# Third attention: GpSimd sets the probabilities above the diagonal to zero for key chunks 1, 2 and 3; TensorE adds the mask for chunk 0 only

## The chip, the cores and the metric

The kernel runs on one core of one Trainium2 chip. The metric is the device time of one execution in microseconds; the time before is the median of three runs.

## The reference

A chain of layers over x (16 sequences of 512 tokens, 128 features): two kinds of attention, a recurrent layer, a Mamba layer, and two mixture-of-experts layers. The change concerns the last attention alone, which computes, for 16 heads of 8 features:

```python
Q, K, V = split_heads(x @ Wq), split_heads(x @ Wk), split_heads(x @ Wv)
Q, K = _rope(Q), _rope(K)
scores = jnp.einsum('bhqd,bhkd->bhqk', Q, K) / jnp.sqrt(jnp.float32(d_k))
causal = jnp.tril(jnp.ones((S, S), dtype=bool))
scores = jnp.where(causal[None, None], scores, -jnp.inf)
attn = jax.nn.softmax(scores, axis=-1)
out = jnp.einsum('bhqk,bhkd->bhqd', attn, V)
return out.transpose(0, 2, 1, 3).reshape(B, S, D) @ Wo
```

The layer behind it is a mixture of 8 experts with the two best chosen for each token. Finding the experts and sending the token rows to them (routing) is done while the attention runs.

## The kernel before

`attend` serves all three attentions. The first has a relative bias and a causal mask, the second is not causal, the third is causal without a bias (`causal and bias is None`); it runs from about 3520 us to 4150 us of the span. The second and third also carry the routing.

A block b is one sequence, a group n = 4b + g (g from 0 to 3) is four heads of it, as two pairs of two heads (r = 0, 1). There are 16 blocks and 64 groups. Scores are held with keys on the partitions and queries along the row. Keys come in four chunks of 128. Because of causality chunk c needs only queries from 128c on, so the causal tiles are: i = 0 chunk 0 (512 wide), i = 1 chunk 1 (384 wide), i = 2 chunk 2 (256) and chunk 3 (128) side by side. In each chunk the first 128 columns are the block on the diagonal, in which half of the entries has to be masked.

A step of TensorE (`step`) does one group. It has six places, at = 3 x pair + i. At each it issues the transposed scores of group n (`scores_t`, L1409) with the mask behind them (L1427), then the plain scores of group n + 2 (`scores_s`, L1376), from which VectorE takes the row maxima (L1758), then one piece of the output of group n - 1 (`pv`, L1448): chunk 0 at the first two places, chunk 1 at the third and fourth, chunk 2 at the fifth, chunk 3 at the sixth. The mask is added by matmuls: identity times a matrix of -1e30 above the diagonal, in two halves of 64 rows, for the two heads side by side on halves of the array.

ScalarE takes the exponential of each tile from PSUM into `probs` (L1668), which is double buffered by group, and counts it in the semaphore `expd`. `pv` waits for the count of the last exponential of its chunk. The exponentials of group n wait for the output of group n - 2.

GpSimd's queue has, block by block: `values(b, g)`, a copy of V (L1303) for each group, and between them the routing of earlier blocks: `locate` (L572 to L582) and the first four scatters (`scatter`, L593, indirect DMAs) after the first `values`, four more scatters, `scale_logits` and `scale_rows` (L545 to L556) after the second, `choose` (L514 to L534) after the third, `stage_x` (L1334) and `parts` (L563, L564) after the fourth. `locate` and `scatter` of b - 3 begin with b = 3, scaling, `choose` and `parts` of b - 2 with b = 2, `stage_x` with b = 1. `parts` waits for ScalarE's logarithm `norm_log`, which is queued in the last step of a block behind its fifth place. SP's queue loads the operands of each group and waits, before it overwrites `v_raw`, for the `values` copy of two groups before.

Of the kernel before, what the change touches and what calls it, by code (L numbers as in the profile page):

```python
# [24 lines left out]
P = 128  # L25
# [1059 lines left out]
def attend(core, x, stacks, v_dram, shift_dram, w, scale, causal, bias=None, routed=None):  # L1085
# [41 lines left out]
    def exp_no(group, pair, i, r):  # L1127
        later = 1 if (pair, i) == LATE else 0
        return USES_OF_GROUP * (group + later) + 2 * EXP_ORDER.index((pair, i)) + r + 1
# [5 lines left out]
        return 2 * len(BY_POOL) * group + 2 * sorted(BY_POOL).index((pair, i)) + r + 1  # L1135

    TURNS = [(0, 1)] if causal else [(0,), (1,)]

    def bank(v, g, pair, i, r):
        return (USES_OF_GROUP * (4 * v + g) + 2 * NTILE * pair + 2 * i + r) % RING  # L1140

    with core.phase() as ph:
# [28 lines left out]
        misc_mm = ph.sem("misc_mm")  # L1171
        misc_read = ph.sem("misc_read")
        rt = Routing(ph, x, *routed) if routed else None
        late_mm = ph.sem("late_mm")
        shift_ready = ph.sem("shift_ready")
        inverted = ph.sem("inverted")
        block = ph.block()
# [108 lines left out]
        @block.gpsimd  # L1286
        def _(pool):

            pool.memset(t_k[:, :, :, :], 1.0).then_inc(zeroed, 1)
            pool.memset(v_st[:, :, :, :, :], 0.0).then_inc(zeroed, 1)  # L1290
            pool.wait_ge(zeroed, 2)
            for two in range(2):
                at = 2 * DK * two + DK
                pool.memset(v_st[:, two, :, :, at:at + 1], 1.0).then_inc(zeroed, 1)
            pool.wait_ge(zeroed, 4)
            pool.sem_inc(v_ready, 2)

            def values(b, g):
                n = 4 * b + g
                pool.wait_ge(v_loaded[g % 2], 16 * (2 * b + g // 2) + 16)  # L1300
                pool.wait_ge(pv_mm, n + 1)
                at = 2 * DK * (g % 2)
                pool.tensor_copy(v_st[:, g % 2, :, :, at:at + DK], v_raw[:, g % 2]).then_inc(v_ready, 1)  # L1303

            def add_bias(b, g, pair, i):

                (_, width, c, first), = tiles[i]
                for r in range(2):
                    j = 2 * pair + r
                    pool.wait_ge(t_copied, pool_no(4 * b + g, pair, i, r))  # L1310
                    tile = probs[:, g % 2, j, tile_at[i]:tile_at[i] + width]
                    pool.tensor_tensor(tile, tile, bias["t_whole"][:, 4 * g + j, first - c * P:first - c * P + width],  # L1312
                                       ALU.add).then_inc(t_biased, 1)

            if not rt:
                for b in range(NB):
                    for g in range(4):
                        values(b, g)
                        for pair, i in sorted(BY_POOL):
                            add_bias(b, g, pair, i)  # L1320
                return
            no = [0]

            def then(ins):
                no[0] += 1
                ins.then_inc(rt.pool_step, 1)
                pool.wait_ge(rt.pool_step, no[0])

            def stage_x(m, added, read):

                pool.wait_ge(misc_read, added + 1)
                if read is not None:
                    pool.wait_ge(misc_mm, read + 1)
                pool.tensor_copy(rt.staged_x[:, :], x[:, T * m:T * m + T]).then_inc(rt.x_staged, 1)  # L1334

            rt.empty_rows(pool)
            for b in range(NB):
                values(b, 0)
                if b >= 3:
                    rt.locate(pool, then, b - 3)  # L1340
                    rt.scatter(pool, b - 3, 0, 4)
                values(b, 1)
                if b >= 3:
                    rt.scatter(pool, b - 3, 4, 8)
                if b >= 2:
                    rt.scale_logits(pool, b - 2)
                    rt.scale_rows(pool, b - 2)
                values(b, 2)
                if b >= 2:
                    rt.choose(pool, then, b - 2)  # L1350
                values(b, 3)
                if b >= 1:
                    stage_x(b - 1, use_no(b, 2, "WO"), use_no(b, 0, "RB") if b >= 2 else None)
                if b >= 2:
                    rt.parts(pool, b - 2)
            rt.locate(pool, then, NB - 3)
            rt.scatter(pool, NB - 3, 0, 8)
            rt.scatter(pool, NB - 2, 0, 8)
            rt.scatter(pool, NB - 1, 0, 8)
            for u in range(RING_ROWS):  # L1360
                pool.wait_ge(rt.sent[u], 16 * TOPK * QT * (NB // RING_ROWS))

        @block.tensor
        def _(pe):
# [31 lines left out]
            def scores_t(b, v, g, pair, i, heads):  # L1396
                if pair == 0 and i == 0 and 0 in heads:
                    pe.wait_ge(t_loaded[g % 2], 96 * (2 * b + g // 2) + 96)
                banks = [bank(v, g, pair, i, r) for r in range(2)]
                for r in heads:  # L1400
                    t_bank_free(b, g, pair, i, r)
                for piece, (at, width, c, first) in enumerate(tiles[i]):
                    last = piece == len(tiles[i]) - 1
                    masked = causal and bias is None and first == c * P
                    parts = 3 if bias is not None and (pair, i) not in BY_DVE | BY_POOL else 0
                    out = [t_ps[:, banks[r], at:at + width] for r in range(2)]
                    for r in heads:
                        rows = slice(HALF * r, HALF * r + ROWS + SHIFT_ROWS)
                        mm = pe.matmul(out[r], t_k[rows, g % 2, pair, c * P:(c + 1) * P],  # L1409
                                       t_q[rows, g % 2, pair, first:first + width],  # L1410
                                       start=True, stop=not masked and not parts)
                        if last and not masked and not parts:
                            mm.then_inc(t_mm, 1)
                    for q in range(parts):
                        for k in range(2):
                            for r in heads:
                                rows = slice(HALF * r, HALF * r + HALF)
                                done = q == 2 and k == 1
                                mm = pe.matmul(out[r], bias["flip"][rows, k],
                                               bias["t"][q][rows, k, 2 * g + pair, first - c * P:first - c * P + width],  # L1420
                                               start=False, stop=done)
                                if last and done:
                                    mm.then_inc(t_mm, 1)
                    for k in range(2 if masked else 0):
                        for r in heads:
                            rows = slice(HALF * r, HALF * r + HALF)
                            mm = pe.matmul(out[r][:, 0:P], w["ident16"][rows, k], w["mask_t"][rows, k],  # L1427
                                           start=False, stop=(k == 1))
                            if last and k == 1:
                                mm.then_inc(t_mm, 1)  # L1430

            def pv(b, k, c, at, to):
                n, g = 4 * b + k, k % 4
                if bias is None and causal and c < 3:
                    pe.wait_ge(expd, exp_no(n, 1, c, 1))
                if not causal and c == 0:
                    pe.wait_ge(expd, USES_OF_GROUP * (n + 1))
                if bias is not None and c < 2:
                    pe.wait_ge(expd, min(max(exp_no(n, pair, c, 1) for pair in range(2)), USES_OF_GROUP * GROUPS + 2))
                if bias is not None and c == 2:  # L1440
                    pe.wait_ge(expd, max(exp_no(n, pair, 2, 1) for pair in range(2)))
                if c == 0:
                    pe.wait_ge(v_ready, 2 + n + 1)
                    if g % 2 == 0:
                        pe.wait_ge(evacuated, 2 * b + g // 2 + 1)
                first = c * P if causal else 0
                for j in range(4):
                    mm = pe.matmul(o_ps[32 * j:32 * j + 32, at:to], v_st[:, g % 2, c, j, :],  # L1448
                                   probs[:, g % 2, j, place[c] + at - first:place[c] + to - first],
                                   start=(g % 2 == 0 and c == 0 and at == 0),  # L1450
                                   stop=(g % 2 == 1 and c == 3 and to == T))
                if c == 3 and to == T:
                    mm.then_inc(pv_mm, 1)
# [1372 lines left out]
```

## Time and profile before

| | us |
|---|---|
| median of three runs | 4495.58 (4492.27 to 4496.21) |
| the profiled execution | 4488.49 |
| its span | 4486.7 |
| busy in the span: TensorE, VectorE, ScalarE, GpSimd | 3969.0, 3190.9, 2844.3, 2366.9 |
| third attention, steady part (3700 to 4050): TensorE, VectorE, ScalarE, GpSimd | 331.6, 307.2, 254.7, 210.0 of 350 |

Busy time of TensorE overlaps with that of its weight loads. Spans of instructions on one engine can overlap their neighbours slightly, so costs in a row are best read from start to start.

### The profile page before, as it was taken

The numbers are of one execution on the slowest core, as the hardware profiler recorded it, in microseconds if no ns is written. First come the engines' busy times: TensorE is split into PE (matmuls) and PEld (weight loads), VectorE is DVE, ScalarE is ACT, GpSimd is POOL, SyncE is SP. The second block draws the span as 40 slices with busy tenths as digits, with TensorE's granted clock in tenths as the row PEclk, the third lists the DMA queues.
The fourth block names the chain that finished last, engine by engine and source line by source line (L and its number), as shares of the span: only waits on it lengthen the run. The fifth ranks groups of instructions, "written<-read, shape, count | busy, mean of one in ns | idle before, by whom it ended". The sixth has DMA issues, their size and how long they took to land. (4 is left out here: it accounts for less than half of the span.)

```text
span 4486.7 us, 91792 instructions
## 1 busy us (share of the span) xinstructions
PE 3969.0 (88%) x30019; PEld 2002.6 (45%) x30020; DVE 3190.9 (71%) x7556; ACT 2844.3 (63%) x5771; POOL 2366.9 (53%) x2903
## 2 busy tenths in 40 slices
PE   7699999899688989889889999997988699996997
PEld 4244444463233333337323333336974244443896
DVE  3588888547899999984479999972126788886013
ACT  7488888767565555547758888873324477775332
POOL 3366666311599999970413444544545246556452
PEclk8799999999899999999979999998989799998997
DMA  9533333104533333310543333325665544442665
GB/s 276 176 90 87 87 88 87 28 0 160 187 131 133 119 126 134 132 64 0 183 148 90 88 89 90 92 68 168 213 207 180 165 112 110 117 113 79 205 213 197
DMA packets 515891, 564.61 MB, mean 126 GB/s; under 512 B 162498, under 2 KB 435523, under 8 KB 507280
## 3 DMA queue, kind: packets, MB, share of 16 engines
q1 hardware_dynamic: 497312, 521.88, 37.9%
q0 software_dynamic: 18160, 37.42, 2.3%
q8 instruction: 229, 3.75, 0.4%
q14 instruction: 190, 1.56, 0.1%
HBM read 399.39 MB, written 159.68 MB: 125 GB/s over the span
## 5 line engine op out<-in xcount | busy, mean ns | idle before, releaser
L1668 ACT ACTIVATE p_probs<-p_t_ps 128x512 f32<-128x512 f32 (+1 forms) x2048 | 1029.4, 557 | 336.2 <-PE p_t_ps L1427 144.9
L1448 PE MATMUL p_o_ps<-p_probs,p_v_st 128*32 128x256 f32 (+3 forms) x9728 | 748.9, 381 | 10.0 <-ACT p_o_sb L1630 9.4
L1761 DVE TENSOR_REDUCE p_row_max<-p_s_ps 128x1 f32<-128x512 f32 x1024 | 632.4, 677 | 51.1 <-PE p_s_ps L1376 51.0
L1376 PE MATMUL p_s_ps<-p_s_k,p_s_q 48*128 48x512 bf16 (+3 forms) x3072 | 607.9, 334 | 52.3 <-DVE p_row_max L1758 36.9
L2492 POOL TENSOR_TENSOR xn<-p_dtx,p_b_sb 128x512 f32<-128x512 f32 x512 | 633.5, 1271 | 34.4 <-DMA p_b_sb<-mamba_rows 17.4
L2564 DVE TENSOR_TENSOR_SCAN p_state<-p_da,xn 128x1024 f32<-128x1024 f32 x256 | 578.8, 2276 | 9.7 <-ACT p_da L2430 7.8
L1409 PE MATMUL p_t_ps<-p_t_q,p_t_k 50*128 50x512 bf16 (+3 forms) x3072 | 546.4, 333 | 36.3 <-ACT p_probs L1668 10.5
L2430 ACT ACTIVATE p_da<-p_dt,p_rate 128x512 f32<-128x512 f32 (+1 forms) x512 | 331.9, 679 | 279.5 <-DVE p_state L2564 277.8
L1758 DVE CUSTOM_DVE_ANT_0 p_tried<-p_s_ps,c_mask_row 128x512 bf16<-128x512 f32 (+3 forms) x1024 | 441.0, 485 | 79.6 <-PE p_s_ps L1376 72.7
L1758 DVE CUSTOM_DVE_ANT_0 p_tried<-p_s_ps,p_s_bias 128x512 bf16<-128x512 f32 (+3 forms) x1024 | 441.4, 481 | 76.0 <-PE p_s_ps L1376 74.4
L1312 POOL TENSOR_TENSOR p_probs<-p_probs,xn 128x384 f32<-128x384 f32 (+1 forms) x384 | 409.1, 1096 | 148.7 <-ACT p_probs L1666 148.3
L802 POOL DMA_INDIRECT weighed_rows<-p_y,p_raw x284 | 272.5, 959 | 290.7 <-DVE p_y L790 246.3
L2340 PE MATMUL p_y_ps<-p_prod,c_ident 128*128 128x512 f32 x832 | 419.5, 627 | 3.8 <-DVE xn L2580 3.7
L790 DVE TENSOR_TENSOR p_y<-p_out_ps,p_raw 128x256 f32<-128x256 f32 x142 | 60.3, 425 | 503.5 <-PE p_out_ps L741 503.5
L772 ACT ACTIVATE p_hidden<-p_hid_ps 128x512 f32<-128x512 f32 x284 | 169.6, 597 | 316.7 <-PE p_hid_ps L730 316.6
L1409 PEld LDWEIGHTS p_t_ps<-p_t_q,p_t_k 50*128 50x128 bf16 x3072 | 166.6, 93 | 445.7 <-ACT p_probs L1668 229.3
L1448 PEld LDWEIGHTS p_o_ps<-p_probs,p_v_st 128*32 128x32 f32 x9728 | 193.9, 108 | 308.4 <-issue 256.1
L1376 PEld LDWEIGHTS p_s_ps<-p_s_k,p_s_q 48*128 48x128 bf16 x3072 | 213.7, 94 | 227.3 <-DVE p_row_max L1761 126.4
L593 POOL DMA_INDIRECT routed_rows<-p_rows,p_index x256 | 252.3, 986 | 99.8 <-issue 72.3
L1303 POOL COPY p_v_st<-p_v_raw 128x128 f32<-128x128 f32 x192 | 56.1, 292 | 439.4 <-PE p_o_ps L1448 251.4
L741 PE MATMUL p_out_ps<-p_wb,p_hidden 128*128 128x128 f32 x2272 | 276.6, 275 | 0.0
L730 PE MATMUL p_hid_ps<-p_xt,p_wb 128*128 128x256 f32 x1136 | 272.6, 384 | 0.0
(318 smaller groups left out, 7018.9 us busy)
## 6 DMA issues: line engine op xcount, KB each, us to landing
p_wb<-in_w SPq DMA_DIRECT2D x142, 512.0 KB, 3.5
p_b_sb<-mamba_rows SPq DMA_DIRECT2D x64, 1024.0 KB
p_s_q<-stack_q SPq DMA_DIRECT2D x384, 96.0 KB, 2.3
p_s_k<-stack_k SPq DMA_DIRECT2D x384, 96.0 KB, 2.4
p_t_q<-stack_q SPq DMA_DIRECT2D x384, 96.0 KB
p_t_k<-stack_k SPq DMA_DIRECT2D x384, 96.0 KB
p_raw<-routed_rows SPq DMA_DIRECT2D x142, 130.0 KB, 3.2
stack_q<-p_parts SPq DMA_DIRECT2D x48, 384.0 KB, 2.6
```

The source lines that it names most:

```text
L741: mm = pe.matmul(out_ps[:, j % 2, c * P:(c + 1) * P], hidden[:, j % 2, f, c * P:(c + 1) * P], wb[:, j % WB, FFN + f * P:FFN + (f + 1) * P] ...
L1312: pool.tensor_tensor(tile, tile, bias["t_whole"][:, 4 * g + j, first - c * P:first - c * P + width], ALU.add).then_inc(t_biased, 1)
L1376: mm = pe.matmul(s_ps[:, slot, at:at + width], s_q[rows, g % 2, pair, c * P:(c + 1) * P], s_k[rows, g % 2, pair, 0:width], start=True, sto ...
L1409: mm = pe.matmul(out[r], t_k[rows, g % 2, pair, c * P:(c + 1) * P], t_q[rows, g % 2, pair, first:first + width], start=True, stop=not mask ...
L1448: mm = pe.matmul(o_ps[32 * j:32 * j + 32, at:to], v_st[:, g % 2, c, j, :], probs[:, g % 2, j, place[c] + at - first:place[c] + to - first] ...
L1668: act.activation(exps, tile, ACT.Exp, scale=scale).then_inc(expd, 1)
L1758: read = dve.tensor_tensor_reduce(tried[:, slot, at:at + width], scores, over, 1.0, LOWEST, ALU.add, ALU.max, found)
L1761: read = dve.tensor_reduce(found, scores, X, ALU.max)
L2340: pe.matmul(y_ps[:, h], w["ident"], prod[:, prod_slot(u, n), half(h)], start=(n == 0), stop=(n == STATE - 1)).then_inc(acc_mm, 1)
L2430: act.activation(da[:, n % RA, h * T + h:h * T + T], dt[:, u, h, h:T], ACT.Exp, scale=rate[:, h, n:n + 1]).then_inc(da_ready, 1)
L2492: pool.tensor_tensor(dbx[:, n % R, half(h)], dtx[:, u, h], b_sb[:, n % RB], ALU.mult).then_inc(dbx_ready, 1)
L2564: dve.tensor_tensor_scan(out=state[:, n % RS], data0=da[:, n % RA], data1=dbx[:, n % R], initial=0.0, op0=ALU.mult, op1=ALU.add).then_inc( ...
```

## The change

For the third attention the diagonal blocks of chunks 1, 2 and 3 (tiles i = 1 and 2, `CLEARED`) are no longer masked before the exponential. GpSimd sets the entries above the diagonal of the finished exponentials to zero with `affine_select`, in place in `probs`, eight instructions for each group: one for each tile i = 1 (128 columns) and one for each tile i = 2 (the two diagonal blocks, 2 x 128 columns), for two pairs and two heads. Each waits for its tile's count in `expd` and counts itself in `cleared`. `clear(n)` stands in GpSimd's queue before the first `values` of the next block (groups 4b - 1) and before the second, third and fourth `values` (groups 4b, 4b + 1, 4b + 2). `pv` of chunk 1 waits for six of the eight, that of chunk 2 for all eight; chunk 3 follows chunk 2. Chunk 0 keeps its mask matmuls.

```diff
+    CLEARED = (1, 2) if causal and bias is None else ()
...
+            def clear(n):
+                if not CLEARED or n < 0:
+                    return
+                for pair, i, r in itertools.product(range(2), CLEARED, range(2)):
+                    pool.wait_ge(expd, exp_no(n, pair, i, r))
+                    last = 2 * (len(tiles[i]) - 1)
+                    blocks = probs[:, n % 2, 2 * pair + r, tile_at[i]:tile_at[i] + (last + 1) * P]
+                    blocks = blocks.rearrange("p (k q) -> p k q", q=P)[:, 0:last + 1:2]
+                    pool.affine_select(blocks, blocks, [[0, len(tiles[i])], [1, P]], ALU.is_ge, 0.0, base=0,
+                                       channel_multiplier=-1).then_inc(cleared, 1)
...
             for b in range(NB):
+                clear(4 * b - 1)
                 values(b, 0)
                 if b >= 3:
                     rt.locate(pool, then, b - 3)
                     rt.scatter(pool, b - 3, 0, 4)
+                clear(4 * b + 0)
                 values(b, 1)
...
+                clear(4 * b + 1)
                 values(b, 2)
                 if b >= 2:
                     rt.choose(pool, then, b - 2)
+                clear(4 * b + 2)
                 values(b, 3)
...
+            clear(GROUPS - 1)
...
-                    masked = causal and bias is None and first == c * P
+                    masked = causal and bias is None and first == c * P and i not in CLEARED
...
-                if bias is None and causal and c < 3:
+                if bias is None and causal and c < 1:
                     pe.wait_ge(expd, exp_no(n, 1, c, 1))
+                if CLEARED and c in CLEARED:
+                    pe.wait_ge(cleared, 8 * n + 4 + 2 * c)
```

GpSimd's order in the third attention, in a late block, from the last instruction of `locate` to the end of the scaling. Before:

```order
L582 COPY p24_rows<-p24_part 128x8
L593 DMA routed_rows<-p24_rows,p24_index 69376x130 x4
L1303 COPY p24_v_st<-p24_v_raw 128x16x8
L593 DMA routed_rows<-p24_rows,p24_index 69376x130 x4
L545 TENSOR_TENSOR p24_logits<-p24_raw,p24_rstd 128x32
L555 TENSOR_TENSOR p24_rows<-p24_raw,p24_rstd 128x4x128 x2
L556 COPY p24_rows<-p24_table_home 128x8
```

After (the `values` copy is now L1304, the select L1338):

```order
L582 COPY p24_rows<-p24_part 128x8
L593 DMA routed_rows<-p24_rows,p24_index 69376x130 x4
L1338 AFFINE_SELECT p24_probs<-p24_probs 128x128 x2
L1338 AFFINE_SELECT p24_probs<-p24_probs 128x2x128 x2
L1338 AFFINE_SELECT p24_probs<-p24_probs 128x128 x2
L1338 AFFINE_SELECT p24_probs<-p24_probs 128x2x128 x2
L1304 COPY p24_v_st<-p24_v_raw 128x16x8
L593 DMA routed_rows<-p24_rows,p24_index 69376x130 x4
L545 TENSOR_TENSOR p24_logits<-p24_raw,p24_rstd 128x32
L555 TENSOR_TENSOR p24_rows<-p24_raw,p24_rstd 128x4x128 x2
L556 COPY p24_rows<-p24_table_home 128x8
```

The eight selects of a group stand between the first four scatters and the `values` copy, behind which come the other four scatters and the scaling. The selects of the next group follow the scaling.

TensorE's order around the third place of a step of the third attention (scores of tile 2, then the first output piece of chunk 1). Before:

```order
L1448 MATMUL p24_o_ps<-p24_probs,p24_v_st 32x256 x4
L1463 MATMUL p24_misc<-c_ident,p24_row_max 16x128
L1409 MATMUL p24_t_ps<-p24_t_q,p24_t_k 128x256 x2
L1427 MATMUL p24_t_ps<-c_mask_t,c_ident16 128x128 x4
L1409 MATMUL p24_t_ps<-p24_t_q,p24_t_k 128x128 x2
L1427 MATMUL p24_t_ps<-c_mask_t,c_ident16 128x128 x4
L1376 MATMUL p24_s_ps<-p24_s_k,p24_s_q 128x256 x2
L1448 MATMUL p24_o_ps<-p24_probs,p24_v_st 32x192 x4
```

After (the lines L1409, L1376, L1448 and L1463 are now L1426, L1393, L1467 and L1482):

```order
L1467 MATMUL p24_o_ps<-p24_probs,p24_v_st 32x256 x4
L1482 MATMUL p24_misc<-c_ident,p24_row_max 16x128
L1426 MATMUL p24_t_ps<-p24_t_q,p24_t_k 128x256 x2
L1426 MATMUL p24_t_ps<-p24_t_q,p24_t_k 128x128 x2
L1393 MATMUL p24_s_ps<-p24_s_k,p24_s_q 128x256 x2
L1467 MATMUL p24_o_ps<-p24_probs,p24_v_st 32x192 x4
```

Two sets of four mask matmuls are gone at this place, and the last row is the first that waits for the selects.

## Rows read from the trace of the kernel before

**Rows 1.** Windows of the third attention: us, busy of PE, PEld, DVE, ACT, POOL; PEclk; DMA

```profile
3700.00:4050.00 350.00, 331.63 (x4683) 163.14 (x4679) 307.17 (x1391) 254.70 (x649) 209.96 (x461) 1.00 0.42 115
...
3536.00:3575.00 39.00, 34.91 (x428) 15.97 (x429) 32.25 (x153) 24.22 (x51) 1.65 (x6) 0.79 0.43 112
...
4105.00:4170.00 65.00, 26.88 (x183) 19.88 (x180) 24.87 (x97) 15.87 (x51) 29.27 (x40) 0.63 0.30 96
```

**Rows 2.** Waits from 3536 to 4107 us: waiter, released by, us in total, times, longest

```profile
ACT p_probs L1668 <- PE p_t_ps L1427: 144.9, 251, 15.8
POOL p_v_st L1303 <- DMA p_v_raw<-values: 111.0, 46, 10.7
PEld p_t_ps L1409 <- ACT p_probs L1668: 104.5, 257, 0.9
POOL p_part_log L563 <- ACT p_norm_log L1611: 77.6, 14, 5.9
```

**Rows 3.** Timeline of TensorE, the last step of a block: start us, us, instruction

```profile
3813.93 0.39 PE L1409 MATMUL p_t_ps<-p_t_q,p_t_k 50*128 50x512 bf16 x2
...
3816.70 0.28 PE L1409 MATMUL p_t_ps<-p_t_q,p_t_k 50*128 50x256 bf16 x2
3816.82 0.28 PE L1427 MATMUL p_t_ps<-c_mask_t,c_ident 64*128 64x128 bf16 x4
3816.93 0.22 PE L1409 MATMUL p_t_ps<-p_t_q,p_t_k 50*128 50x128 bf16 x2
...
3817.31 0.53 PE L1448 MATMUL p_o_ps<-p_probs,p_v_st 128*32 128x192 f32 x8
...
3823.66 0.39 PE L1409 MATMUL p_t_ps<-p_t_q,p_t_k 50*128 50x512 bf16 x2
```

**Rows 4.** Timeline of GpSimd: one `locate` five blocks earlier, then one block

```profile
3644.11 1.05 POOL L572 TENSOR_TENSOR p_base<-p_base,p_counts 128x8 f32<-128x8 f32 x4 [0.53 <-ACT p_counts L1570]
...
3805.95 0.29 POOL L1303 COPY p_v_st<-p_v_raw 128x128 f32<-128x128 f32 x1 [0.17 <-DMA p_v_raw<-values]
...
3813.92 0.20 POOL L534 TENSOR_TENSOR p_behind<-p_best 128x4 f32<-128x4 f32 x1
...
3815.00 0.29 POOL L1303 COPY p_v_st<-p_v_raw 128x128 f32<-128x128 f32 x1 [0.87 <-DMA p_v_raw<-values]
3815.23 0.62 POOL L1334 COPY p_staged_x<-x 128x512 f32<-128x512 f32 x1
...
3821.26 0.20 POOL L563 TENSOR_TENSOR p_part_log<-p_behind,p_norm_log 128x4 f32<-128x4 f32 x1 [5.41 <-ACT p_norm_log L1611]
...
3824.50 1.05 POOL L572 TENSOR_TENSOR p_base<-p_base,p_counts 128x8 f32<-128x8 f32 x4
...
3828.05 0.20 POOL L582 COPY p_rows<-p_part 128x8 f32<-128x8 f32 x1 [0.47 <-ACT p_part L1618]
3829.07 1.06 POOL L593 DMA_INDIRECT routed_rows<-p_rows,p_index  x1 [0.82 <-POOL p_rows L582]
...
3833.92 0.31 POOL L1303 COPY p_v_st<-p_v_raw 128x128 f32<-128x128 f32 x1
...
3841.39 0.19 POOL L556 COPY p_rows<-p_table_home 128x8 int32<-128x8 int32 x1
```

**Rows 5.** GpSimd groups by shape, whole span: count, busy us, mean ns, idle before

```profile
L1303 POOL COPY p_v_st<-p_v_raw 128x128 f32<-128x128 f32 x192 | 56.1, 292 | 439.4 <-PE p_o_ps L1448 251.4 <-DMA p_v_raw<-values 187.8
...
L516 POOL TENSOR_SCALAR p_ahead<-p_differ 128x256 f32<-128x256 f32 x28 | 24.4, 870 | 2.5
...
L518 POOL TENSOR_TENSOR p_differ<-p_differ,p_table_earlier 128x256 f32<-128x256 f32 x28 | 20.4, 729 | 2.3
...
L1334 POOL COPY p_staged_x<-x 128x512 f32<-128x512 f32 x30 | 18.5, 617 | 0.8 <-DVE x L1814 0.6
...
L525 POOL TENSOR_SCALAR p_is_rank<-p_rank 128x32 f32<-128x32 f32 x56 | 16.1, 288 | 4.8
...
L521 POOL TENSOR_TENSOR p_half<-p_ahead 128x128 f32<-128x128 f32 x28 | 12.8, 457 | 2.2
```

More of the change, by code:

```diff
@@ L1173, in attend @@
         rt = Routing(ph, x, *routed) if routed else None
-        late_mm = ph.sem("late_mm")
+        late_mm, cleared = ph.sem("late_mm"), ph.sem("cleared")
         shift_ready = ph.sem("shift_ready")
```

## Prediction

> **What bounds the kernel now.** Only the third attention changes, so I read its stretch. Of the window table, the three rows in [rows 1] are the steady part, the start and the tail of this attention. In the steady part TensorE is busy 331.6 of 350 us (95%) at a granted clock of 1.00, VectorE 307.2, ScalarE 254.7 and GpSimd 210.0. The list of waits over the whole attention [rows 2] agrees: ScalarE waits 144.9 us for the mask matmuls of L1427, while weight loads of L1409 wait 104.5 us for exponentials, which is time that mostly lies beside running matmuls. TensorE sets the pace, with VectorE 8% behind it. GpSimd looks free: 40% idle. But its idle time is of one kind only, and that decides this case. Per block of four groups it is the wait for `norm_log` (77.6 us over 14 blocks), a wait for the `values` load, and gaps between its DMA issues, which are not free time.
>
> The pace: the first `base` addition of `locate` starts at 3644.11 and, five blocks later, at 3824.50 [rows 4]. That is 180.4 / 5 = 36.1 us for a block, 9.0 for a group.
>
> **What TensorE saves.** In the step at [rows 3] the two 256-wide score matmuls start at 3816.70, their masks at 3816.82, the next scores at 3816.93: four mask matmuls (two halves of the identity, two heads side by side) cost 0.11 us. A group has eight such sets, two for each key chunk; six go. That is 6 x 0.11 = 0.66 us of a group's 9.0, so a TensorE step of 8.4, and 64 x 0.66 = 42 us at the most, if nothing else becomes late. VectorE's 307.2 of 350 is 31.7 us of a 36.1 us block, still below 4 x 8.4 = 33.4, so it would not stop this gain.
>
> **What GpSimd gets.** Each group adds eight selects, four over 128x128 and four over 2x128 columns. No row shows such an instruction, so I bound the mean cost c of one (start to start) by what GpSimd does on float32 of these widths [rows 5]. From below: the copy, 0.292 us for 128 columns and 0.617 for 512, by interpolation 0.40 for 256, mean 0.35; back to back the next instruction starts some 0.05 before such a span ends (0.23 after the copy at 3815.00, [rows 4]), so c = 0.30. From above, within the rows: TENSOR_SCALAR with a comparison, 0.870 for 256 columns and 0.288 for 32, so 0.54 for 128, mean 0.70, c = 0.65. Between them TENSOR_TENSOR, 0.457 for 128 and 0.729 for 256, mean 0.59, c = 0.54. A select reads one operand, but makes a comparison value for each element and chooses by it, so I hold it nearer to the dearer rows and take c = 0.54. It could be dearer than all of them, since it also counts the positions; I keep 0.8 as the outer end.
>
> One sentence of the Trainium skill, "GPSIMD Engine Reference", section 4.1 (Engine selection), says that one-input elementwise work on GpSimd runs at roughly line rate; by that c would be the copy's 0.30 and the sum below about +22 us. The row speaks against its use here: the one-input comparison takes (0.870 - 0.288) / 224 = 2.6 ns for a column against the copy's (0.617 - 0.292) / 384 = 0.85.
>
> **Where the selects lie.** GpSimd runs its queue in order. The output matmuls of group n-1 for chunk 1 are issued at the third place of step n and now wait for the sixth select of group n-1, those for chunks 2 and 3 at the fifth place for the eighth. In the step of [rows 3] that third place is 3.4 us in (3813.93 to 3817.31). Selects of a group can't end before its exponentials, about when the next step begins, so GpSimd has only some 3 us in which it must be free, once in each step. Its old work is queued right in front of them: behind the change a block reads `values`, `locate`, four scatters, select group 4b; `values`, four scatters, scaling, select 4b+1; `values`, `choose`, select 4b+2; `values`, `stage_x`, `parts`, select 4b+3. Work that had 36 us to be done in is now waited for three times in a block.
>
> I follow one block around from S, the end of the sixth select of group 4b+2, at which TensorE goes on at the third place of the last step. Durations are from [rows 3, 4].
> - TensorE and ScalarE until `parts` can run: 3821.26 - 3817.31 = 3.95, less one mask set, 3.8; `parts` itself 0.4. The last two selects, `values` and `stage_x` hide in it (2 x 0.54 + 0.9 = 2.0). Together 4.2.
> - Eight selects of group 4b+3: 8c.
> - `values` 0.25, `locate` to its first scatter 3829.07 - 3824.50 = 4.57 less its 0.47 of waiting, 4.1; four scatters 3833.92 - 3829.07 = 4.85. Together 9.2.
> - Eight selects of group 4b: 8c. The sixth comes S + 4.2 + 9.2 + 14c = S + 21.0; TensorE without waiting would be there at S + 6.0 (3823.66 - 3817.31, less three mask sets) + 8.4 + 3.1 (the 3.4 to the third place, less three) = S + 17.5. It waits 3.5 us.
> - `values`, four scatters and scaling: 3841.58 - 3833.92 = 7.7. Then 8c. That leg is 12.0 where a TensorE step is 8.4: 3.6 us of waiting.
> - `values` and `choose`: 3814.12 - 3805.95 = 8.2 (the last row's start and its 0.20). Then 6c of group 4b+2, which is the next S. Again 12.5 against 8.4.
>
> The sum is 29.3 + 30c. With c = 0.54 a block takes 45.5 us instead of 36.1: +9.4. The chain is closed by GpSimd alone except for its first 3.8 us, so the 0.66 us of each TensorE step is lost in it, all but the one mask set counted. Scatters run from block 3 on: 13 blocks, 13 x 9.4 = +122 us. Of the eleven steps before the first S, TensorE saves 11 x 0.66 = 7 us, and block 2, which already has scaling and `choose`, gives back about 4 in its two waits: -3. The tail is as it was (24 scatters behind the last selects, [rows 1] third row, TensorE idle); I give it 0. ScalarE and VectorE are not charged. SP's queue waits for `values` before it reloads `v_raw`; each `values` now comes up to a step later, behind the selects of the group before, but still before the SP step that asks for it, so 0; were it late, the loads of t_q would be next and TensorE with them, which I leave to the upper end.
>
> Total: 122 - 3 = +119. The profiled execution took 4488.5 us (span 4486.7), which lies 7.1 below the median of the runs, 4495.6. So 4488.5 + 119 = 4607.5, and for the median 4615. At c = 0.30 a block is 38.3, +2.2, 13 x 2.2 = 29, with the full 7 saved ahead: +22, 4517. At c = 0.65: 48.8, 13 x 12.7 - 3 = +162, 4658. At c = 0.8: 13 x 17.2 - 3 = +221, 4717. No change of pace at 29.3 + 30c = 36.1, c = 0.23.
>
> **Rivals.**
> - Faster: the selects fit. It decides at c = 0.23, no more than the 128-column copy's own spacing of 0.23, and four of eight selects are twice as wide. For it speaks the 40% of idle GpSimd [rows 1]; against it that the chain above counts every gap and that a select can hardly beat a copy. If it all fitted: -42 us, 4453. Chance 0.07, and 0.04 for the narrow band around no change.
> - Cheap selects, at the copy's rate, c up to 0.42: TensorE loses what it saved and some; +22 to +72, about 4545. Chance 0.22.
> - My forecast, c from 0.42 to 0.68: +72 to +174. Chance 0.47.
> - Dear selects, or TensorE's clock. This stretch was granted 1.00, the 2.4 GHz level, throughout; at the start of this attention, where TensorE waits for loads and maxima, it is 0.79, and in the tail, where it mostly idles, 0.63 [rows 1]. Waits of 3 to 4 us three times a block may bring the 1.2 GHz level into the steady part. Most of that would be hidden by the waits themselves, but the 3.8 us leg in front of `parts` is on the chain and could double: 13 x 3.5 = +45, about 4660. With c near 0.8 the same. Chance 0.20.
> - That the masks don't go, or something else is added: the order of instructions shows 24 mask matmuls fewer in each step and eight selects more; no chance left for it.
>
> **How the numbers follow.** Likeliest 4615. The range leaves out about 0.1 on each side: below, the faster case and the cheapest selects, 4515; above, c over 0.79 or half clock on top of 0.65, 4710. About 0.2%, 9 us, is what a measurement here can tell from no change. Faster 0.07, same 0.04, slower 0.89.
>
> **What would show it.** In the new profile: mask matmuls at 512 instead of 2048; selects whose mean over the two widths is near 0.6 us; GpSimd busy over 85% of the steady stretch; blocks of about 45 us between first `base` additions; TensorE's output matmuls waiting for GpSimd's selects in three steps of four, not in the step after `parts`, and hardly at all in blocks 0 and 1, where steps should be 8.4 us. Wrong would be: selects under 0.25 us, waits in every step alike, or a block much longer than 29.3 + 30c, which would mean a link that I have left out (the clock, the reloading of `v_raw`, or GpSimd and VectorE slowing each other).

## The result, and the profile after

The change made the kernel slower: 4537.3 us median of four runs (4532.2 to 4541.9) against 4493.9, ratio 1.0096 with an interval of 1.0083 to 1.0109, or +43 us. A second measurement beside the later experiments gave 1.0103 (1.0088 to 1.0119). The direction and the mechanism were forecast, the size (+119) was not.

The profiled execution took 4541.9 us, span 4540.2, that is 53.5 more than the span before. Of these, 7.7 had come up before GpSimd's first routing instruction of this attention (3549.8 against 3542.1), in code that the change does not touch. I take them for scatter between executions: the first weighed-row scatter of the first expert layer (L802) starts at 3081.9 against 3076.2 here, and between 3076.2 and 3082.3 over the fourteen traces of this document. The line of busy times, and the window that answers to the first of [rows 1]:

```profile
PE 3987.0 (88%) x28483; PEld 1973.4 (43%) x28484; DVE 3189.1 (70%) x7556; ACT 2844.3 (63%) x5771; POOL 2518.5 (55%) x3415
```

```profile
3700.00:4050.00 350.00, 308.04 (x3397) 130.17 (x3395) 280.21 (x1265) 229.84 (x584) 275.80 (x702) 0.93 0.38 103
```

TensorE fell from 331.6 to 308.0 us busy of 350, GpSimd rose from 210.0 to 275.8, and the granted clock fell from 1.00 to 0.93. The selects, by shape in the same window, to be held against [rows 5]:

```profile
L1338 POOL TENSOR_SCALAR_AFFINE_SELECT p_probs<-p_probs 128x256 f32<-128x256 f32 x140 | 53.2, 401 | 0.0
L1338 POOL TENSOR_SCALAR_AFFINE_SELECT p_probs<-p_probs 128x128 f32<-128x128 f32 x140 | 37.6, 288 | 0.1
```

They take 0.29 and 0.40 us, the copy's own times (0.292, and 0.40 by interpolation). Eight in a row take 2.43 us from start to start, so c = 0.304. Waits from 3560 to 4150 us, as in [rows 2]:

```profile
ACT p_probs L1687 <- PE p_t_ps L1444: 100.5, 96, 3.1
...
PEld p_o_ps L1467 <- POOL p_probs L1338: 49.4, 44, 2.4
POOL p_part_log L563 <- ACT p_norm_log L1630: 41.8, 13, 4.0
PE p_o_ps L1467 <- POOL p_probs L1338: 40.6, 35, 2.2
POOL p_probs L1338 <- ACT p_probs L1687: 30.0, 31, 2.0
...
POOL p_v_st L1304 <- DMA p_v_raw<-values: 10.1, 9, 2.1
```

The output matmuls now wait for GpSimd. GpSimd's own waiting for the load of `values` has gone from 111.0 us in [rows 2] to 13.0 in the stretch that answers to it, 3544 to 4160; between 3700 and 4050 it has gone from 28.0 to nothing. The 30.0 us in which the selects wait for exponentials lie in the first three blocks; between 3700 and 4050 there are none. GpSimd's timeline over two blocks, which answers to [rows 4]:

```profile
3806.69 1.04 POOL L572 TENSOR_TENSOR p_base<-p_base,p_counts 128x8 f32<-128x8 f32 x4
...
3836.59 2.48 POOL L1338 TENSOR_SCALAR_AFFINE_SELECT p_probs<-p_probs 128x128 f32<-128x128 f32 x8
3839.02 0.29 POOL L1304 COPY p_v_st<-p_v_raw 128x128 f32<-128x128 f32 x1
3839.25 0.61 POOL L1346 COPY p_staged_x<-x 128x512 f32<-128x512 f32 x1
3842.08 0.20 POOL L563 TENSOR_TENSOR p_part_log<-p_behind,p_norm_log 128x4 f32<-128x4 f32 x1 [2.22 <-ACT p_norm_log L1630]
...
3845.11 1.04 POOL L572 TENSOR_TENSOR p_base<-p_base,p_counts 128x8 f32<-128x8 f32 x4
...
3877.49 0.29 POOL L1304 COPY p_v_st<-p_v_raw 128x128 f32<-128x128 f32 x1
...
3882.37 0.20 POOL L563 TENSOR_TENSOR p_part_log<-p_behind,p_norm_log 128x4 f32<-128x4 f32 x1 [4.04 <-ACT p_norm_log L1630]
...
3885.39 1.04 POOL L572 TENSOR_TENSOR p_base<-p_base,p_counts 128x8 f32<-128x8 f32 x4
```

One block is 38.42 us, the next 40.28, and so they alternate nearly throughout: the 13 intervals between the 14 first `base` additions have a mean of 39.30, where before it was 35.70. Of these 39.30, GpSimd is busy 32.96 and has 2.8 of gaps at its scatters; it waits 3.19 for `norm_log` and 0.32 for ScalarE's `part` in `locate`, and for nothing else. The wait for `norm_log` is 2.2 us in the shorter block, 4.0 in the longer. What differs is TensorE's clock in that leg. Its timeline, from the first output piece of chunk 1 in the last step of either block:

```profile
3838.40 0.53 PE L1467 MATMUL p_o_ps<-p_probs,p_v_st 128*32 128x192 f32 x8 [1.08 <-POOL p_probs L1338]
...
3841.06 0.64 PE L1467 MATMUL p_o_ps<-p_probs,p_v_st 128*32 128x256 f32 x8
...
3876.87 0.87 PE L1467 MATMUL p_o_ps<-p_probs,p_v_st 128*32 128x192 f32 x8 [2.23 <-POOL p_probs L1338]
...
3881.55 1.08 PE L1467 MATMUL p_o_ps<-p_probs,p_v_st 128*32 128x256 f32 x8
```

In the shorter block, after a wait of 1.08 us, the matmuls run at the 2.4 GHz level (0.53, 0.64); in the longer one, after a wait of 2.23 us, at 1.2 GHz (0.87, 1.08), until 3882.6. From that first piece to `parts` it is 3.68 us in the one and 5.50 in the other, which is the 1.8 us by which the blocks differ.

The shorter block has the half level too, but one step earlier, where TensorE waits for the next selects again. The same pieces of chunk 1 in the step before, first of the shorter block, then of the longer:

```profile
3827.88 0.72 PE L1467 MATMUL p_o_ps<-p_probs,p_v_st 128*32 128x192 f32 x8 [1.41 <-POOL p_probs L1338]
...
3829.71 0.87 PE L1467 MATMUL p_o_ps<-p_probs,p_v_st 128*32 128x192 f32 x8
...
3866.34 0.53 PE L1467 MATMUL p_o_ps<-p_probs,p_v_st 128*32 128x192 f32 x8 [1.42 <-POOL p_probs L1338]
```

Waits of 1.41 and 1.42 us stand in front, and only the first is followed by the half level. The alternation is not a fixed feature of the kernel: in a second profiled execution of the change the wait for `norm_log` also lies between 2.2 and 4.0 us, but mostly in between, and the mean block is 39.20.

### The profile page after: what moved, and what is told of

Its sections match the earlier page's. It is cut to its first block and busy times, and to the rows that moved or that the text cites. A ratio compares the mean times of both kernels' runs of the same rounds, so it can differ in the third digit from the quotient of the medians.

```text
span 4540.2 us, 89233 instructions
## 1 busy us (share of the span) xinstructions
PE 3987.0 (88%) x28483; PEld 1973.4 (43%) x28484; DVE 3189.1 (70%) x7556; ACT 2844.3 (63%) x5771; POOL 2518.5 (55%) x3415
## 5 line engine op out<-in xcount | busy, mean ns | idle before, releaser
L1467 PE MATMUL p_o_ps<-p_probs,p_v_st 128*32 128x256 f32 (+3 forms) x9728 | 763.4, 387 | 53.2 <-POOL p_probs L1338 42.9
L1393 PE MATMUL p_s_ps<-p_s_k,p_s_q 48*128 48x512 bf16 (+3 forms) x3072 | 637.9, 339 | 54.8 <-DVE p_row_max L1777 37.3
L2511 POOL TENSOR_TENSOR xn<-p_dtx,p_b_sb 128x512 f32<-128x512 f32 x512 | 633.0, 1271 | 34.8 <-DMA p_b_sb<-mamba_rows 17.9
L1426 PE MATMUL p_t_ps<-p_t_q,p_t_k 50*128 50x512 bf16 (+3 forms) x3072 | 537.5, 337 | 30.0 <-ACT p_probs L1687 8.9
L802 POOL DMA_INDIRECT weighed_rows<-p_y,p_raw x284 | 271.9, 957 | 291.9 <-DVE p_y L790 247.5
L1467 PEld LDWEIGHTS p_o_ps<-p_probs,p_v_st 128*32 128x32 f32 x9728 | 196.0, 109 | 359.7 <-issue 250.9
L1426 PEld LDWEIGHTS p_t_ps<-p_t_q,p_t_k 50*128 50x128 bf16 x3072 | 155.6, 93 | 447.4 <-ACT p_probs L1687 217.0
L1393 PEld LDWEIGHTS p_s_ps<-p_s_k,p_s_q 48*128 48x128 bf16 x3072 | 227.0, 96 | 260.9 <-DVE p_row_max L1780 126.4
L741 PEld LDWEIGHTS p_out_ps<-p_wb,p_hidden 128*128 128x128 f32 x2272 | 264.9, 192 | 0.1
```

The lines of the kernel that those rows point to most:

```text
L741: mm = pe.matmul(out_ps[:, j % 2, c * P:(c + 1) * P], hidden[:, j % 2, f, c * P:(c + 1) * P], wb[:, j % WB, FFN + f * P:FFN + (f + 1) * P] ...
L1393: mm = pe.matmul(s_ps[:, slot, at:at + width], s_q[rows, g % 2, pair, c * P:(c + 1) * P], s_k[rows, g % 2, pair, 0:width], start=True, sto ...
L2511: pool.tensor_tensor(dbx[:, n % R, half(h)], dtx[:, u, h], b_sb[:, n % RB], ALU.mult).then_inc(dbx_ready, 1)
```

## The experiments

Times are against the kernel before on the same chip. "Block" is the mean of the 13 intervals between first `base` additions in the profiled execution. "No masks, no selects" leaves out the masking of chunks 1 to 3 altogether.

| kernel | ratio (95% interval) | us | block |
|---|---|---|---|
| before | | | 35.70 |
| the change, again | 1.0103 (1.0088 to 1.0119) | +45 | 39.20 |
| masks kept as well | 1.0129 (1.0113 to 1.0144) | +56 | 39.75 |
| selects twice | 1.0384 (1.0368 to 1.0400) | +170 | 47.87 |
| two scatters moved | 1.0002 (0.9993 to 1.0011) | +1 | 35.88 |
| no masks, no selects | 0.9969 (0.9957 to 0.9982) | -14 | 34.99 |
| only tile 2 cleared | 0.9969 (0.9957 to 0.9981) | -14 | 34.82 |

**GpSimd's chain, stretched.** Each group's selects were done a second time:

```diff
-                for pair, i, r in itertools.product(range(2), CLEARED, range(2)):
+                for again in range(2):
+                    for no, (pair, i, r) in enumerate(itertools.product(range(2), CLEARED, range(2))):
...
-                    pe.wait_ge(cleared, 8 * n + 4 + 2 * c)
+                    pe.wait_ge(cleared, 16 * n + 12 + 2 * c)
```

> Each group's eight selects are done twice (the second pass changes nothing; TensorE waits for the second). Theory A: the block is 29.3 + 60 x 0.304 = 47.5 us, 9.1 more than the change, 13 x 9.1 = +118 and a few us in block 2: about +120 over the change, +165 over before; with the 1.2 GHz level after longer waits up to 45 us more. Rival B, that GpSimd has slack left and the change's loss comes from where TensorE has to wait rather than from how long GpSimd works: well under +80 over the change.

Measured +170, and the first `base` additions of one block and the next:

```profile
3801.15 1.06 POOL L572 TENSOR_TENSOR p_base<-p_base,p_counts 128x8 f32<-128x8 f32 x4
...
3848.93 1.05 POOL L572 TENSOR_TENSOR p_base<-p_base,p_counts 128x8 f32<-128x8 f32 x4
```

The blocks are 47.75 to 47.82 us, the last alone 48.94, against 47.5 from the formula. The selects are on the path one by one. The granted clock of the steady window was 0.87, and yet the block is no longer than the sum. TensorE's output pieces of chunk 1, and two of chunk 2 (256 wide), in three steps on end:

```profile
3814.33 0.87 PE L1470 MATMUL p_o_ps<-p_probs,p_v_st 128*32 128x192 f32 x8 [5.01 <-POOL p_probs L1341]
...
3826.80 0.53 PE L1470 MATMUL p_o_ps<-p_probs,p_v_st 128*32 128x192 f32 x8 [2.26 <-POOL p_probs L1341]
...
3829.46 1.08 PE L1470 MATMUL p_o_ps<-p_probs,p_v_st 128*32 128x256 f32 x8
...
3839.78 0.53 PE L1470 MATMUL p_o_ps<-p_probs,p_v_st 128*32 128x192 f32 x8 [2.30 <-POOL p_probs L1341]
...
3842.44 0.64 PE L1470 MATMUL p_o_ps<-p_probs,p_v_st 128*32 128x256 f32 x8
```

The half level (0.87, 1.08) falls into the first two legs, after which TensorE waits for the selects again anyway. The leg in front of `parts`, from 3839.78 on, runs at 2.4 GHz.

**GpSimd's chain, shortened where it was idle.**

```diff
-                    rt.scatter(pool, b - 3, 4, 8)
+                    rt.scatter(pool, b - 3, 4, 6)
...
                     stage_x(b - 1, use_no(b, 2, "WO"), use_no(b, 0, "RB") if b >= 2 else None)
+                if b >= 3:
+                    rt.scatter(pool, b - 3, 6, 8)
```

> The change with two of the second four scatters moved from in front of the selects of group 4b+1 to the last slot of the block, between stage_x and parts, where GpSimd waits 2.2 to 4.0 us for norm_log. Theory A, the chain of GpSimd: that slot grows to 0.6 + 0.9 + 0.2 + 2.5 + 0.4 = 4.6 us, the other shrinks by 2.5: 27.2 + 30 x 0.304 = 36.3 us a block, 2.1 less than 38.4; and the alternating 1.6 us, TensorE's half level in front of parts, is hidden behind the scatters. 13 x 0.6 - 2 = +6 us over before, some 37 us faster than the change. Rival, that only the sum of GpSimd's work counts or that waits at fixed places cost in themselves: as the change, +43.

Measured +1: 44 us came back by moving two scatters into the wait for `norm_log`, which fell from 3.2 us a block to 0.1. The clock of its steady window is 1.00 again. No select was saved and none got cheaper (0.288 and 0.400 us), so what the change lost could be had back by the order of GpSimd's queue alone. GpSimd now works almost without a break, busy 33.1 us and 2.7 of gaps at its scatters in a block of 35.9, and TensorE still waits for its selects 17 times between 3700 and 4050, 10.5 us in all. With the move the change is as fast as the kernel before, not faster.

**TensorE's part alone.** The masks of chunks 1 to 3 left out and no selects (`clear` returns at once, `pv` waits for `expd`).

> The masks of key chunks 1 to 3 left out and nothing in their place (leaves out the masking of these diagonal blocks; output not the reference's). It measures what TensorE's part is worth alone. Theory A: TensorE is the bound of the kernel before, six sets of 0.11 us in each of 64 steps: -42 us, block 35.7 - 2.6 = 33.1 us, granted clock still 1.00. Rival: VectorE (31.7 us of a block) with ScalarE's and the misc bank's waits is next at once: half of it, about -20 us.

Measured -14: the rival, and less than it said. So even free selects could not have brought 42 us. Its waits from 3700 to 4050 us:

```profile
PEld p_t_ps L1426 <- DMA p_t_q<-shifts: 15.0, 18, 1.9
PEld p_s_ps L1393 <- DVE p_row_max L1777: 11.4, 47, 0.6
```

Before the change these were 9.5 and 0.5 in the same window. The shifts are the row maxima with their sign turned, which go through a store and a load before they stand in `t_q` for the transposed scores. I took VectorE for the cause first.

**The change with its masks kept.** `masked = causal and bias is None and first == c * P`, selects as in the change.

> The change with all mask matmuls kept as well (the selects then clear entries that are zero already). Theory A, GpSimd's queue sets the block: at the measured 0.304 us a select a block is 29.3 + 30 x 0.304 = 38.4 us whatever TensorE does beside it, against 35.7 before, so +13 x 2.7 = +35 us over the kernel before; and since TensorE's gaps are filled with mask matmuls again, the drops of its granted clock (0.93 in the steady part of the change, every second block 40.2 us instead of 38.4) become fewer: +35 to +43, not slower than the change's +43. Rival B, TensorE's 0.66 us a group still counts in the change: this run is slower than the change by up to 42 us, +85 over before.

Measured +56, between both theories. Its blocks are 0.45 to 0.55 us longer than the change's, some 6 to 7 us in all; the rest of the 11 us is about as large as the uncertainty of two ratios from different chips. Theory B is out, theory A misses some 15 us: TensorE's work is not fully beside the chain. The traces tell what carries the 0.55 us a block over the second profile of the change: GpSimd waits 0.58 us a block for ScalarE's `part` in `locate` instead of 0.28, and 3.32 for `norm_log` instead of 3.16, and is busy 0.1 us longer. The granted clock was 0.96 in its steady window, higher than with the change (0.93 and 0.94), so more drops of the clock are not the reason.

**Half of the selects.** `CLEARED = (2,)`, with the counts of `cleared` to match.

> Only tile 2 (chunks 2 and 3) is cleared by GpSimd, four selects of 0.35 us start to start for each group; chunk 1 keeps its mask matmuls, so four of the six sets go. Theory A: GpSimd's chain is 29.3 + 15 x 0.35 = 34.6 us, below the 35.7 of before, TensorE's own block 35.7 - 1.8 = 33.9: block 34.6, 13 x -1.1 and three blocks of -1.8: -20 us against before, granted clock 1.00. Rival B, waits for GpSimd at fixed places cost whatever its load: slower than before.

Measured -14, block 34.8. From 3700 to 4050 us TensorE has no wait for GpSimd. But it is only what leaving out all masks brings, so something at 35.0 us a block was holding both.

**What holds 35.0 us.** VectorE's maxima were spread otherwise, on top of two kernels:

```diff
         s_tiles = [[(0, 512, 3)], [(0, 128, 0), (128, 384, 2)], [(0, 256, 1)]]
+        if bias is None:
+            s_tiles = [[(0, 512, 3)], [(0, 384, 2)], [(0, 256, 1), (256, 128, 0)]]
```

> As the kernel that clears only tile 2 (measured -14), with VectorE's maxima spread otherwise: query chunk 0 (128 keys) goes from the second and fifth place of the step to the third and sixth. Theory V, which explains why taking the masks away alone gave -14 and not -42: at the second and fifth place the four maxima of two heads take 2 x (0.21 + 0.48) = 1.38 us, as long as TensorE's place of 1.28 us, so time saved there is waited away for VectorE; moved, they take 0.96 there and 1.10 instead of 0.69 in the other. Then GpSimd's chain, 34.6 us, is next, against 35.0 now: about -20 over before. Rival, loads of shifted rows or ScalarE hold the block at 35.0: -14 again.

> Masks of chunks 1 to 3 and selects left out (output not the reference's), with the same new spread of VectorE's maxima. Theory V: TensorE's saving comes through, block near 33.5 us instead of 35.0, about -35 us over before (-14 without the new spread). Rival: -14 again.

Measured 0.9976 (0.9967 to 0.9985) and 0.9966 (0.9954 to 0.9978), -11 and -15: as the same kernels without it. Theory V alone fell, by the medians. The profiled execution of the first was the fastest of its eleven (4473.9 us, median 4483.1), with blocks of 33.9 us instead of 34.8; what the other ten did was not traced. The second's block was 34.56. The second one's waits, its timeline of TensorE at the start of a step and SP's queue in that step tell what came in its place:

```profile
PEld p_t_ps L1428 <- DMA p_t_q<-shifts: 27.3, 31, 2.2
```

```profile
3806.63 0.39 PE L1428 MATMUL p_t_ps<-p_t_q,p_t_k 50*128 50x512 bf16 x2 [1.52 <-DMA p_t_q<-shifts]
...
3815.24 0.39 PE L1428 MATMUL p_t_ps<-p_t_q,p_t_k 50*128 50x512 bf16 x2 [0.32 <-DMA p_t_q<-shifts]
```

```profile
3811.45 0.31 SPq L1248 DMA_DIRECT2D shifts<-p_shift  x1
3813.35 0.55 SPq L1236 DMA_DIRECT2D p_t_q<-shifts  x2
```

VectorE's shifts go out 4.8 us into the step, are loaded again 1.9 us after the issue of the store, and the step of the next group starts 1.9 us after the issue of that load: 8.6 us for a step, and its block is 4 x 8.64. So the transpose of the row maxima (`MT`), from which VectorE makes the shifts, was issued at the first place of the step instead of the second:

```diff
         misc_at = dict(MT=1, OT=3, WO=5, BT=5, RA=5, RB=5)
+        if bias is None:
+            misc_at["MT"] = 0
```

> Masks of chunks 1 to 3 and selects left out (output not the reference's), with the new spread of VectorE's maxima and with the transpose of the row maxima (MT) at the first place of a step instead of the second. Theory D, on why taking the masks away gave only -14: the shifts of group n+1 must go from VectorE through a store and a load before step n+1 can start. In the run with the new spread alone shift_low ended 4.8 us into the step, its store was issued at once and the operand was there 3.8 us later, 8.6 us for a step, and TensorE waited for it 31 times in 350 us. One place earlier is 1.3 us earlier: TensorE sets the step again at 8.4, block 33.5, -35 over before. Rival: something else holds it at 34.9, -15 again.

> The same with the new spread of VectorE's maxima as well. Theories V and D together (each alone gains nothing since the other is next): block 33.9, TensorE's own with four of six mask sets gone, -28 over before. Rival: -14.

> Only tile 2 cleared by GpSimd, two scatters moved to the last slot, MT one place earlier, VectorE's maxima as in the kernel before. GpSimd's chain: slot with parts 2 x 0.35 + 0.9 + 2.5 + 0.4 = 4.5, then 9.2 + 5.2 + 8.2 and 14 selects of 0.35 = 32.0 us, no bound. Theory D: the step is freed from the shifts' way through memory: block 34.3, -22 over before. Rival, VectorE at the second and fifth place or something else: -14 as without it.

> The kernel before with MT one place earlier only. TensorE waited for the shifts 9.5 and 2.0 us of 350 there: at most 11.5 / 350 x 560 = 18 us, likelier half of it since these are waits of weight loads beside matmuls: -5 to -10. Rival, that the shifts don't matter: 0 or slower, since TensorE waits for the maxima and the misc bank at its first place.

"Both moves" are the new spread of VectorE's maxima and the early transpose.

| kernel | ratio (95% interval) | us | block |
|---|---|---|---|
| no masks, no selects; both moves | 0.9929 (0.9916 to 0.9943) | -32 | 33.52 |
| tile 2 cleared, scatters moved; both moves | 0.9933 (0.9920 to 0.9947) | -30 | 33.54 |
| tile 2 cleared, scatters moved; early transpose only | 0.9988 (0.9979 to 0.9997) | -5 | 35.38 |
| before; early transpose only | 0.9995 (0.9986 to 1.0004) | -1 | |

Without masks and selects the new spread gave 1 us on top of the -14, and with the early transpose as well it gave 18. In the third kernel of the table, which has the early transpose with the old spread, the weight loads of the plain scores wait for VectorE 117 times, 30.2 us of 350 (46 times, 11.4 us, with tile 2 cleared alone), and the gain is -5 where -22 was expected (-14 was the rival). The likely reason, not shown by itself, is that the transpose needs VectorE's last maxima sooner. On the kernel before, the early transpose gave -1 where -5 to -10 was expected. The two theories hold together only: with both moves -32 came where -35 was expected, and -30 where -28 was. The second kernel of the table does the whole masking and beats both the kernel before and the change. The kernel before with both moves was not run, so how much of the 30 us the moves would give with all masks kept is open. The steady window of the second kernel:

```profile
3700.00:4050.00 350.00, 341.68 (x4306) 157.65 (x4304) 323.03 (x1474) 268.44 (x684) 282.58 (x660) 1.00 0.45 121
```

TensorE is busy 341.7 of 350 there, GpSimd 282.6, more than in the change, and no other engine waits for it in this window.

## Why the prediction was right in its sign and wrong in its size

- **TensorE bounds, 95% busy: only half true.** The mask sets cost 0.11 us each, as read (from the first score matmul of the third place to its plain scores it is 0.40 us before, 0.18 after, with two sets gone), and mask matmuls went from 2048 to 512. But "42 us if nothing else becomes late" was the wrong price: -14. I compared busy sums of a block (VectorE 31.7 against 33.4) and did not look at the places of a step, nor at the way of the shifts through memory, whose waits of 9.5 us stand in the same window before. In the sum this term was only 7 us, because I had TensorE's saving lost behind GpSimd; the rival "faster, 4453" was priced on it and, by the run without selects, could not have come true.
- **The chain: right.** 29.3 + 30c gives 38.4 at the measured c, the shorter blocks are 38.4; with 60 selects 47.5 against 47.8; with the scatters moved 36.3 against 35.9. Leg by leg, the fixed parts were forecast as 4.2, 9.2, 7.7 and 8.2 us; in the block of 38.42 they are 4.0, 9.6, 7.6 and 8.1, so the sum of 29.3 holds in part because the second, in which `locate` waits 0.4 us for `part`, was too small and the others too large. TensorE waits for the selects in three steps of four (24 waits of matmuls and 25 of weight loads in some nine blocks from 3700 to 4050 us).
- **c: the step that failed.** I took 0.54 from the rows of two-input and comparing instructions; it was 0.304, the copy's rate, my lower end. 13 x 30 x (0.54 - 0.304) = 92 us too much. The rule that I had set aside, that one-input elementwise work on GpSimd runs at roughly line rate (the Trainium skill, "GPSIMD Engine Reference", section 4.1), agrees with the select's rows, (0.401 - 0.288) / 128 = 0.88 ns for a column, and its sum of +22 was nearer than mine. The row by which I rejected it, the comparison with 2.6 ns for a column, is of another instruction. What came was my rival of cheap selects (+22 to +72), to which I had given 0.22.
- **The pace before.** 36.1 us from five blocks; all 13 intervals give 35.7, because three of my five were 36.2 or more, one of them, 37.17, the longest of all. 13 x 0.4 = 5 us too little.
- **The clock.** Forecast as a rival, "the leg in front of `parts` could double", for 45 us. It does lengthen just that leg, by at most 1.8 us instead of 3.5, and fully only in every second block: (39.3 - 38.4) x 13 = 12 us. I had it outside the likeliest case.
- **Together.** 13 x (38.4 - 35.7) = 35, the clock 12, and 1.5 gained before block 3 (6.2 us late at the first `base` addition, 7.7 at the start of GpSimd's work): 46 us in the profile and nothing more in the tail (53.0 late at GpSimd's last `base` addition, 53.5 at the end). The medians say 43. The smaller misses went the other way: the pace 5 us, the clock 12 and the credit ahead of block 3 (3 forecast, 1.5 measured) took back some 18 of the 92 us that c was too dear, so that the total is nearer than c itself was, by luck.
- **Looked for and seen:** GpSimd was 79% busy, not over 85%, since selects were cheaper and the gaps at scatters aren't busy time. Its late `values` cost nothing that shows: TensorE's matmuls and weight loads wait 3.4 us for the shifts from 3700 to 4050, 11.5 before. That GpSimd and VectorE might slow each other did not show either: GpSimd's 256-wide comparison took 0.87 us and VectorE's 512-wide maximum 0.69, as before.

## What to carry to other kernels

An engine that is 40% idle can still be full: count what stands in its queue between two instructions that others wait for, gaps of its DMA issues included, and write the loop as a sum with the new cost as a variable. Then the loop says where work may go for free, and moving two scatters gave back what the whole change had lost. Before pricing a saving on the busiest engine, look for the second row in the list of waits, also where it is small: a cut of 0.66 us in a step met a way through memory and a place of VectorE that were each 0.2 to 0.3 us behind (steps of 8.75 and 8.64 us against 8.93).

## What the runs showed of the hardware

- An affine select on GpSimd, float32 in place, takes the time of a copy: 0.288 us for 128 columns, 0.401 for 2 x 128, and 0.30 on average from start to start.
- TensorE's waits for the selects, in three steps of four, were enough to bring it down to 1.2 GHz for parts of the steady stretch (granted clock 0.93 with the change, 0.87 with selects twice). Such waits don't bring it about in every case: with two scatters moved, matmuls waited for selects 17 times from 3700 to 4050, none over 1.1 us, and the clock was 1.00. The length of the wait just before doesn't decide it alone: 1.41 and 2.23 us stood in front of the half level with the change, while after 1.42 us with the change, and after 2.30 us with selects twice, it stayed at 2.4 GHz. What does decide it wasn't settled. What it cost was decided by the leg that it fell into: 1.8 us in front of `parts`, nothing in the legs whose end TensorE waits for in any case.
